# Adaptive layer norm, attention head and quantised product: the head's biases and matrices prepared elsewhere, the bias product moved, modulation rows spread from a copy

## Chip, cores and metric
One core of one Trainium2 chip. The metric is the device time of one execution in microseconds. Before the change: median 370.23 us over 3 runs (369.77 to 370.35).

## What is computed
The input x is (8, 1024, 512) in float32, eight samples of 1024 rows. The reference, cut to what matters:

```
mod = (silu(c) @ wmod).reshape(8, 6, 1, 512)
sa, ca, ga, sb, cb, gb = mod[:, 0..5]
ga, gb = sign(g) * max(|g|, 0.25) for each
h = layernorm(x) * (1 + ca) + sa
x = x + ga * attention(h)              # q, k, v, three passes, out @ Wo.T + bo
h = layernorm(x) * (1 + cb) + sb
x = x + gb * (mx_quantize(h) @ mx_quantize(weight).T + bias)
```

The attention writes only the first 16 of each sample's 1024 rows with something other than zero (before its output projection). So for all other rows the first step adds `ga * bo`, called v. The 128 first rows (16 of each of 8 samples) are "the head", and are worked apart. The quantiser divides blocks of 32 numbers by a scale and rounds each to a small grid.

## The kernel before
**Tiling.** x is handled in 16 groups of 4 tiles of 128 rows (`GROUPS`, `TILES`), two groups a sample. Tile q runs from 0 to 63. For each group: v is added (groups 0 and 1 on VectorE and GpSimd, from group 2 on by an accumulating DMA from GpSimd's queue, `sum_by_dma`, line 346); ScalarE makes sums, deviations and the normalised U (`sums`, `deviations`, `normalise`); GpSimd modulates, U * c + sb (`modulate`, lines 370 and 377, two tiles at a time); VectorE takes block maxima, quantises to Q8 and, for the early groups, multiplies back into DD (`maxima`, `block_scales`, `to_grid`, `from_grid`). TensorE turns a tile of DD (`transposes`, line 660), ScalarE copies its high part XH, VectorE subtracts the low part XL, and TensorE makes the product: the bias row first (line 675), eight matmuls with XH, four with XL. VectorE adds the result to x (`add_tile`, line 1162) and SyncE stores it. The weights are scaled by each sample's gate gb on GpSimd (`scale_weights`), turned by TensorE (`weight_turn`, line 623) at the tiles in `FOLDS` (3 to 6 for sample 1), and split into WH (ScalarE) and WL (VectorE, line 1114).

**The order.** Each engine has its queue written out by hand: the start, then `for q in range(LAST)`. At tile q TensorE does `transposes(q + 1)`, `product(q)`, `head_work(q)` and a weight turn. VectorE does `add_tile(q - 1)`, `low_part(q + 1)`, `weight_low`, the group steps that are due (`due(q, lead)`), and `head_work(q)` last. GpSimd has no tiles; it goes by group: `modulate(g)`, later `from_grid(g - 1)`, `scale_weights`, `sum_by_dma(g + 3)`.

**The start.** `silu(c)` goes to TensorE. There `spread(i, bank, signal)` multiplies a broadcast column of it with a block of wmod, so that sample 0's row of modulation stands in all 128 partitions of a PSUM bank (used for v, c and sb), and `rows_of` makes the rows of all 8 samples (8 partitions). ScalarE copies these to `msp`, and SyncE writes them to `mod_scratch` in HBM, from where later samples' rows are broadcast. c and sb of sample 0 are read by VectorE from PSUM (`first_modulate`, tiles 0 and 1) and by GpSimd from ScalarE's copies c_bc and sb_bc (tiles 2 and 3). c's rows are made inside tile 0 (`head_work(0)`), sb's at the end of the start. `gate_bias_rows` splits the bias rows of all samples into a high and low part, G, ahead of `first_modulate`.

**The head.** `head_work(q)` interleaves the head's chain. On VectorE: tile 1 makes `bias_rows` (rows of the three small layers' biases, 4 steps on one partition), tiles 2 and 3 the head's own norm, tile 4 `centre_diagonals`, which subtracts from two block-diagonal matrices in BD their mean over columns (line 948 reduction, 949 mean, 952 four 32x32 blocks each). They are first used at tile 9. On TensorE the projections to v, q and k stand in tiles 6, 7 and 8 (line 763).

Of the kernel before, what the change touches and what calls it, by code (L numbers as in the profile page):

```python
# [15 lines left out]
P = 128  # L16
# [6 lines left out]
HALF = 2  # L23
# [15 lines left out]
def build(nc, x, xh, WqT, WkT, WvT, WoT, bo, lna, BDs, rows, columns, masks, w, cT, wmod, ident, out):  # L39
# [4 lines left out]
    with ExitStack() as ctx:  # L44
# [110 lines left out]
        V_BANK, GATE_ROWS, COLUMN_ROWS, C_BANK, S_BANK, LATE_ROWS = 0, 6, 1, 2, 3, 7  # L155
# [26 lines left out]
        bd_done, hs_sa = sem("bd_done"), sem("hs_sa")  # L182
# [50 lines left out]
        def _(sp):  # L233
# [41 lines left out]
            sp.wait_ge(rows_cp, 3)  # L275
# [3 lines left out]
            sp.wait_ge(rows_cp, 4)  # L279
# [45 lines left out]
        def _(pool):  # L325
# [65 lines left out]

            add_attn_bias(1)
# [6 lines left out]
            for g in range(1, GROUPS):  # L399
# [5 lines left out]
                if g + 3 < GROUPS:  # L405
                    sum_by_dma(g + 3)
            from_grid(GROUPS - 1)

        @block.scalar
        def _(act):  # L410
# [146 lines left out]
            copy_rows(sb_rows, LATE_ROWS, 3)  # L557
# [4 lines left out]
            for q in range(LAST):  # L562
# [9 lines left out]
                if q == 1:  # L572
                    copy_rows(c_rows_all, LATE_ROWS, 4, 1.0)
# [8 lines left out]
        def _(pe):  # L582
# [3 lines left out]
            def spread(i, bank, signal):  # L586
                for k in range(NC):
                    pe.wait_ge(wmod_in[6 if i == 0 and k < HALF else i], 16)
                    m = M(ps[:, bank, :], cE[:, k, 0:1].to_broadcast([P, P]), mod_w[i][:, k, :],
                          start=k == 0, stop=k == NC - 1)  # L590
                m.then_inc(signal, 1)
# [35 lines left out]
            spread(0, V_BANK, ga_mm)  # L627
# [8 lines left out]
            spread(2, C_BANK, c_mm)  # L636
            pe.wait_ge(gb_col, 1)
            for n in range(NC):
# [3 lines left out]
            spread(3, S_BANK, s_mm)  # L642
            pe.wait_ge(blq_cp, 1)
            rows_of(3, LATE_ROWS)
# [18 lines left out]
            def product(n):  # L663
# [11 lines left out]
                M(bank, pick[:, b:b + 1].to_broadcast([P, P]), G[:], start=True, stop=False)  # L675
                pe.wait_ge(xh_done, n + 1)
                for k in range(NC):
                    r = slice(k * P, (k + 1) * P)
                    M(bank, XH[:, n % 2, r], WH[:, b % 2, k, :], start=False, stop=False)  # L679
                    M(bank, XH[:, n % 2, r], WL[:, b % 2, k, :], start=False, stop=False)  # L680
                pe.wait_ge(xl_done, n + 1)
                for k in range(NC):
                    r = slice(k * P, (k + 1) * P)
                    m = M(bank, XL[:, n % 2, r], WH[:, b % 2, k, :], start=False, stop=k == NC - 1)  # L684
                m.then_inc(y_done, 1)
# [19 lines left out]
            def attend(i, o):  # L705
                if o == 0:
# [3 lines left out]
                    if i == 0:  # L710
                        pe.wait_ge(lrow_done, 4)
                        pe.wait_ge(cleared, 5)
                        pe.wait_ge(bd_done, 1)
# [555 lines left out]
```

## Time and profile before
| what | value |
|---|---|
| median of 3 runs | 370.23 us (369.77 to 370.35) |
| the profiled execution | 371.03 us, its span 369.1 us, 6369 instructions |
| TensorE (PE) busy | 330.8 us, 90% |
| VectorE (DVE) busy | 290.8 us, 79% |
| ScalarE (ACT) busy | 223.0 us, 60% |
| GpSimd (POOL) busy | 216.9 us, 59% |
| mean granted clock of TensorE | 0.976 |
| share of the chain that ended last | PE 43%, DVE 36%, ACT 10%, issue 8% |

Times in a timeline are microseconds from the span's start. A row of a timeline gives the start, the time taken, the engine, the line of the kernel, the operation, what it writes and reads, and how many such instructions it stands for; in brackets stands how long the engine was idle before it, and what ended that. A matmul of float32 is two instructions. "Issue" in the chain is time in which an engine waited for nothing that the profile shows.

### The profile page before, as it was taken

The page shows a single profiled execution, that of the slowest core. Times are in us where ns is not written, and L with a number is a line of the kernel's source. Part 1 is how long each engine was busy: PE and PEld are TensorE (multiplying, and loading weights), DVE is VectorE, ACT ScalarE, POOL GpSimd, SP SyncE. Part 2 cuts the span into 40 slices and gives each one's busy share as a digit, 9 for nine tenths or more (in the row PEclk, how much of TensorE's full clock was granted, in tenths as well). Part 3 has the DMA queues.
Part 4 walks back from the last instruction along what each step waited for, and adds up shares of the span by engine and source line. Part 5 has one row for each costly group of instructions (what it writes and reads, how often), then busy time and mean ns, then how long its engine had stood idle before and what let it go on. Part 6 is the DMA issues. An engine that isn't in the chain of part 4 may idle for free.

```text
span 369.1 us, 6369 instructions
## 1 busy us (share of the span) xinstructions
PE 330.8 (90%) x2334; PEld 251.7 (68%) x2334; DVE 290.8 (79%) x508; ACT 223.0 (60%) x505; POOL 216.9 (59%) x131
## 2 busy tenths in 40 slices
PE   3987999549999799989999999989999989995894
PEld 1232556438988686777888678768877877684783
DVE  4799949998448996879798689896976989699732
ACT  3367654765756867786778588948593875121210
POOL 2068392462886679559967796898684767402000
PEclk9999899997999999999999999999998999998999
DMA  7989999975197727965697669768681982020122
GB/s 219 404 333 360 295 231 223 322 269 100 69 201 175 186 114 134 265 101 197 150 275 194 174 135 262 179 168 170 230 198 37 222 174 115 3 99 17 67 103 85
DMA packets 22933, 66.93 MB, mean 181 GB/s; under 512 B 2371, under 2 KB 2500, under 8 KB 18934
## 3 DMA queue, kind: packets, MB, share of 16 engines
q1 hardware_dynamic: 15360, 51.83, 41.8%
q0 software_dynamic: 7392, 14.68, 24.2%
q8 instruction: 18, 0.29, 0.3%
q14 instruction: 13, 0.11, 0.1%
q10 hardware_dynamic: 150, 0.02, 0.0%
HBM read 49.39 MB, written 17.14 MB: 180 GB/s over the span
## 4 chain that ended last, share of the span: by engine, by line
PE 43%; DVE 36%; ACT 10%; issue 8%; DMA 1%; DVEq 0%; SPq 0%; ACTq 0%
PE ps L679 7%; PE ps L680 7%; PE ps L684 7%; DVE XL L1107 5%; PE ps L660 4%; DVE Q L1148 4%; DVE WL L1114 3%; DVE amax L1129 3%; ACT U L447 3%; PE ps L763 3%; DVE X L1162 3%; PE ps L623 3%; DVE DD L1155 3%; ACT XH L430 2%; ACT unused L460 2%
## 5 line engine op out<-in xcount | busy, mean ns | idle before, releaser
L370 POOL TENSOR_TENSOR U<-U,c_bc 128x1024 f32<-128x1024 f32 x31 | 75.6, 2439 | 48.3 <-ACT U L447 48.2
L679 PE MATMUL ps<-WH,XH 128*128 128x512 f32 x256 | 103.4, 404 | 0.3 <-ACT XH L430 0.3
L680 PE MATMUL ps<-WL,XH 128*128 128x512 f32 x256 | 103.0, 402 | 0.0
L430 ACT ACTIVATE XH<-ps 128x512 fp32r<-128x512 f32 x64 | 37.8, 591 | 84.8 <-PE ps L660 84.6
L1107 DVE TENSOR_TENSOR XL<-ps,XH 128x512 fp32r<-128x512 f32 x64 | 43.9, 686 | 52.8 <-ACT XH L430 52.7
L377 POOL TENSOR_TENSOR U<-U,sb_bc 128x1024 f32<-128x1024 f32 x31 | 74.1, 2389 | 4.5 <-POOL U L370 0.2
L684 PE MATMUL ps<-WH,XL 128*128 128x512 f32 x256 | 68.8, 390 | 0.0
L447 ACT ACTIVATE U<-X,nmr,rstd 128x512 f32<-128x512 f32 x64 | 48.2, 807 | 24.7 <-DVE nmr L1122 21.5
L680 PEld LDWEIGHTS ps<-WL,XH 128*128 128x128 f32 x256 | 49.9, 195 | 11.5
L679 PEld LDWEIGHTS ps<-WH,XH 128*128 128x128 f32 x256 | 50.1, 196 | 9.5 <-ACT XH L430 0.6
L684 PEld LDWEIGHTS ps<-WH,XL 128*128 128x128 f32 x256 | 48.4, 189 | 10.5
L1162 DVE TENSOR_TENSOR X<-ps,X 128x512 f32<-128x512 f32 x64 | 43.6, 681 | 8.1 <-PE ps L684 7.8
L471 ACT ACTIVATE unused<-X,negm 128x512 bf16<-128x512 f32 x64 | 45.6, 715 | 0.5
L660 PE MATMUL ps<-idf,DD 128*128 128x128 f32 x256 | 40.0, 281 | 3.6 <-DVE WL L1114 3.1
L460 ACT ACTIVATE unused<-X 128x512 bf16<-128x512 f32 x64 | 39.4, 617 | 0.1
L1148 DVE TENSOR_TENSOR Q<-U,ps 128x1024 fp8e4<-128x1024 f32 x32 | 39.0, 1217 | 0.2
L1129 DVE TENSOR_REDUCE amax<-U 128x32 f32<-128x1024 f32 x32 | 38.7, 1209 | 0.0
L660 PEld LDWEIGHTS ps<-idf,DD 128*128 128x128 f32 x256 | 31.4, 146 | 8.3 <-DVE WL L1114 3.4
L356 POOL TENSOR_TENSOR DD<-Q,s 128x1024 f32<-128x1024 fp8e4 x12 | 23.0, 1916 | 23.4 <-DVE Q L1148 21.8
L675 PE MATMUL ps<-G,pick 128*128 128x512 f32 x64 | 31.3, 490 | 0.6 <-DVE X L1162 0.6
L346 POOL DMA_DIRECT2D X<-mod_scratch x14 | 18.5, 1325 | 17.5 <-DMA X<-in_x 12.7
L389 POOL TENSOR_SCALAR Wb<-Wd,TA 128x512 f32<-128x512 f32 x28 | 18.9, 691 | 12.8 <-PE ps L623 8.3
(219 smaller groups left out, 447.9 us busy)
## 6 DMA issues: line engine op xcount, KB each, us to landing
X<-in_x SPq DMA_DIRECT2D x16, 1024.0 KB, 8.5
out<-X SPq DMA_DIRECT2D x15, 1024.0 KB, 5.7
X<-mod_scratch POOLq DMA_DIRECT2D x14, 1024.0 KB, 12.8
X<-in_wmod SPq DMA_DIRECT2D x2, 1024.0 KB, 14.1
sb_bc<-mod_scratch SPq DMA_DIRECT2D x7, 256.0 KB, 12.1
c_bc<-mod_scratch SPq DMA_DIRECT2D x7, 256.0 KB, 10.5
X<-in_wmod SPq DMA_DIRECT2D x2, 512.0 KB, 4.7
Wd<-in_w SPq DMA_DIRECT2D x1, 1024.0 KB, 10.0
```

What stands on the lines that cost most here:

```text
L370: nc.gpsimd.tensor_tensor(a, a, spread(c_bc[:, b % 2, :]), ALU.mult).then_inc(u_done, 2 if g == 0 else 1)
L377: nc.gpsimd.tensor_tensor(a, a, spread(sb_bc[:, b % 2, :]), ALU.add).then_inc(h_done, 2 if g == 0 else 1)
L447: A.activation(U[:, g % 2, j, :], X1[:, g % XSLOTS, j, :], ACT.Identity, bias=nmr[:, g % 2, j:j + 1], scale=rstd[:, g % 2, j:j + 1]).then_ ...
L460: A.activation(unused[:, j % 2, :], X1[:, g % XSLOTS, j, :], ACT.Identity, accum_out=total[:, j:j + 1]).then_inc(sum_done, 1)
L660: m = TR(ps[:, XT_BANK + n % 2, c * P:(c + 1) * P], DD[:, j, c * P:(c + 1) * P], idf[:])
L679: M(bank, XH[:, n % 2, r], WH[:, b % 2, k, :], start=False, stop=False)
L680: M(bank, XH[:, n % 2, r], WL[:, b % 2, k, :], start=False, stop=False)
L684: m = M(bank, XL[:, n % 2, r], WH[:, b % 2, k, :], start=False, stop=k == NC - 1)
L1107: TT(XL[:, n % 2, :], ps[:, XT_BANK + n % 2, :], XH[:, n % 2, :].bitcast(F32), ALU.subtract).then_inc(xl_done, 1)
L1129: RED(amax[:, h, :], blocks(U[:, g % 2, HALF * h:HALF * (h + 1), :]), AX, ALU.max, apply_absolute_value=True).then_inc(am_done, 1)
L1148: TT(blocks(Q8[:, h]), blocks(U[:, g % 2, HALF * h:HALF * (h + 1), :]), wide(inv[:, h, :]), ALU.mult, saturate=False).then_inc(q_done, 1)
L1162: TT(a, ps[:, Y_BANK + n % 2, :], a, ALU.add).then_inc(o_done, 1)
```

## The change
- `bias_rows` moves on VectorE from tile 1 to the start, behind `early_constants`.
- `centre_diagonals` is split: VectorE makes the two means at tile 4 (`diagonal_means`), and GpSimd subtracts them, in 8 steps, behind the modulation of group 1 and the DMA for group 4, ahead of the modulation of group 2.
- A tile's bias product comes last in its sum; only tile 0 waits for G there. `gate_bias_rows` moves behind `low_part(0)`.
- The rows of c are made in the start, copied with 1 added, and sb's behind them into the same bank. c and sb of sample 0 are spread from the copies, with one matmul each.
- Banks: the column rows go from bank 1 to 7, rows of c and sb from 7 to 6. SyncE's wait for the copied rows stands once, earlier.

```diff
-            sp.wait_ge(rows_cp, 3)
+            sp.wait_ge(rows_cp, 4)
             sp.dma_start(mod_dram[SB], sb_rows).then_inc(sb_out, 16)
             sp.wait_ge(wt_mm, NC)
             sp.dma_start(Wb[:], chunked(WqT)).then_inc(wq_in, 16)
-            sp.wait_ge(rows_cp, 4)
...
+            def centre_diagonals():
+                for n, i in enumerate((0, 2)):
+                    pool.wait_ge(bdm_done, n + 1)
+                    for q in range(4):
+                        r = slice(32 * q, 32 * q + 32)
+                        nc.gpsimd.tensor_scalar(BD[r, i, r], BD[r, i, r], bdm[r, n:n + 1], 1.0,
+                                                ALU.subtract, ALU.mult).then_inc(bd_done, 1)
+                        pool.wait_ge(bd_done, 4 * n + q + 1)
...
                 if g + 3 < GROUPS:
                     sum_by_dma(g + 3)
+                if g == 1:
+                    centre_diagonals()
...
             deviations(0, 1)
+            copy_rows(c_rows_all, CS_ROWS, 3, 1.0)
             act.wait_ge(rows_turned, 1)
             A.copy(column_rows, ps[0:COLUMNS * B, COLUMN_ROWS, :]).then_inc(columns_cp, 1)
             normalise(0, 0)
+            copy_rows(sb_rows, CS_ROWS, 4)
             act.wait_ge(c_mm, 1)
-            A.activation(c_bc[:, 0, :], ps[:, C_BANK, :], ACT.Identity, bias=1.0).then_inc(c_rows, 1)
+            A.copy(c_bc[:, 0, :], ps[:, C_BANK, :]).then_inc(c_rows, 1)
             normalise(0, 1)
             act.wait_ge(s_mm, 1)
             A.copy(sb_bc[:, 0, :], ps[:, S_BANK, :]).then_inc(s_rows, 1)
             sums(1, 0)
             for k in range(NC):
                 weight_high(0, k, W_FIRST_BANKS[k])
-            copy_rows(sb_rows, LATE_ROWS, 3)
...
+            def spread(rows, bank, n, signal):
+                pe.wait_ge(rows_cp, n)
+                M(ps[:, bank, :], idf[0:B, 0:1].to_broadcast([B, P]), rows, start=True, stop=True).then_inc(signal, 1)
...
-            spread(2, C_BANK, c_mm)
+            rows_of(2, CS_ROWS)
             pe.wait_ge(gb_col, 1)
+            pe.wait_ge(blq_cp, 1)
             for n in range(NC):
                 m = TR(ps[0:COLUMNS * B, COLUMN_ROWS, n * P:(n + 1) * P],
                        TA[:, n, :, :].rearrange("p w b -> p (w b)"), idf[:])
             m.then_inc(rows_turned, 1)
-            spread(3, S_BANK, s_mm)
-            pe.wait_ge(blq_cp, 1)
-            rows_of(3, LATE_ROWS)
+            pe.wait_ge(rows_cp, 3)
+            rows_of(3, CS_ROWS)
+            spread(c_rows_all, C_BANK, 3, c_mm)
+            spread(sb_rows, S_BANK, 4, s_mm)
...
-                M(bank, pick[:, b:b + 1].to_broadcast([P, P]), G[:], start=True, stop=False)
                 pe.wait_ge(xh_done, n + 1)
...
+                if n == 0:
+                    pe.wait_ge(g_rows, 3)
+                M(bank, pick[:, b:b + 1].to_broadcast([P, P]), G[:], start=False, stop=True).then_inc(y_done, 1)
...
                 if q == 0:
                     pe.wait_ge(c_heads, 1)
                     pe.wait_ge(wt_low, NC)
-                    pe.wait_ge(rows_cp, 3)
-                    rows_of(2, LATE_ROWS)
                     head_rows(4, CA_BANK)
...
             pe.wait_ge(v_row, 1)
-            pe.wait_ge(columns_cp, 1)
-            pe.wait_ge(g_rows, 3)
+            pe.wait_ge(rows_cp, 4)
             for k in range(NC):
                 weight_turn(0, k, W_FIRST_BANKS[k])
...
-            def centre_diagonals():
+            def diagonal_means():
                 dve.wait_ge(bd_in, 16)
                 for n, i in enumerate((0, 2)):
                     link(RED(bdm[:, n:n + 1], BD[:, i, :], AX, ALU.add))
-                    link(TS(bdm[:, n:n + 1], bdm[:, n:n + 1], 1.0 / HD, None, ALU.mult))
-                    for q in range(4):
-                        r = slice(32 * q, 32 * q + 32)
-                        link(TS(BD[r, i, r], BD[r, i, r], bdm[r, n:n + 1], None, ALU.subtract))
-                W_.memset(dn[:, 4:5], 0.0).then_inc(bd_done, 1)
+                    TS(bdm[:, n:n + 1], bdm[:, n:n + 1], 1.0 / HD, None, ALU.mult).then_inc(bdm_done, 1)
...
-                STT(a, spread(C_BANK), 1.0, a, ALU.add, ALU.mult).then_inc(u_first, 1)
+                TT(a, spread(C_BANK), a, ALU.mult).then_inc(u_first, 1)
...
             early_constants()
+            bias_rows()
             first_v()
...
             quantise(Wd[:, HALF:NC, :], Q8[:, 1], HALF * NB).then_inc(wd_done, 1)
-            gate_bias_rows()
             first_modulate()
...
             low_part(0)
+            gate_bias_rows()
             maxima(0, 1)
```

## Rows read from the trace of the kernel before

**Rows 1.** The page's groups of instructions; after the bar busy us, mean ns, idle us before.
```profile
L679 PE MATMUL ps<-WH,XH 128*128 128x512 f32 x256 | 103.4, 404 | 0.3 <-ACT XH L430 0.3
...
L389 POOL TENSOR_SCALAR Wb<-Wd,TA 128x512 f32<-128x512 f32 x28 | 18.9, 691 | 12.8 <-PE ps L623 8.3
```

**Rows 2.** Chain of waits, 24 to 124 us, in order of time: start us, us, what.
```profile
28.21 0.68 DVE G L917
...
52.29 1.14 DVE amax L1129
...
55.21 1.42 DVE LR L941
...
57.37 0.46 DVE LR L941
...
58.57 0.69 DVE X L1162
```

**Rows 3.** The centring's line on VectorE: ns min/median/max, first and last start us.
```profile
L952 DVE TENSOR_SCALAR BD<-BD,bdm x8: 229/270/2320, 73.8 to 80.5; 32x32 f32<-32x32 f32 x8
```

**Rows 4.** VectorE's timeline, 73 to 89 us: start us, us, engine, line, operation.
```profile
73.34 0.27 DVE L948 TENSOR_REDUCE bdm<-BD 128x1 f32<-128x128 f32 x1
...
80.93 0.69 DVE L1162 TENSOR_TENSOR X<-ps,X 128x512 f32<-128x512 f32 x1
...
82.73 1.21 DVE L1129 TENSOR_REDUCE amax<-U 128x32 f32<-128x1024 f32 x1
...
87.89 1.22 DVE L1155 TENSOR_TENSOR DD<-Q,ps 128x1024 f32<-128x1024 fp8e4 x1
```

**Rows 5.** TensorE's timeline, 82 to 111 us, same columns.
```profile
82.96 0.45 PE L623 MATMUL ps<-idf,odd 128*128 128x128 f32 x1 [5.33 <-DVE WL L1114]
...
89.40 3.74 PE L763 MATMUL ps<-msp,early 128*128 128x128 f32 x32
...
93.41 0.60 PE L660 MATMUL ps<-idf,DD 128*128 128x128 f32 x4
...
109.91 1.08 PE L684 MATMUL ps<-WH,XL 128*128 128x512 f32 x4
```

**Rows 6.** Busy us by stretch; TensorE's granted clock stands after the POOL column.
```profile
83.00:88.00 5.00, 5.00 (x16) 4.32 (x17) 4.86 (x11) 1.09 (x2) 0.00 (x0) 0.50 0.97 178
```

**Rows 7.** TensorE's timeline, 21 to 38 us.
```profile
21.67 3.70 PE L589 MATMUL ps<-X,cE 128*128 128x512 f32 x8 [0.41 <-DMA X<-in_wmod]
...
29.18 3.60 PE L596 MATMUL ps<-U,cE 128*8 128x512 f32 x8
...
37.82 1.97 PE L660 MATMUL ps<-idf,DD 128*128 128x128 f32 x8 [3.15 <-DVE WL L1114]
```

**Rows 8.** ScalarE's timeline, a pair of normalisations and a pass of one tile.
```profile
28.23 1.50 ACT L447 ACTIVATE U<-X,nmr,rstd 128x512 f32<-128x512 f32 x2
...
99.52 0.61 ACT L460 ACTIVATE unused<-X 128x512 bf16<-128x512 f32 x1
```

**Rows 9.** VectorE's timeline, 11 to 32 us.
```profile
11.81 0.69 DVE L902 TENSOR_SCALAR odd<-ps 128x512 f32<-128x512 f32 x1 [2.88 <-PE ps L589]
...
29.63 1.22 DVE L959 SCALAR_TENSOR_TENSOR U<-ps,U 128x1024 f32<-128x1024 f32 x1
30.88 1.22 DVE L962 TENSOR_TENSOR U<-U,ps 128x1024 f32<-128x1024 f32 x1
```

**Rows 10.** GpSimd's timeline, 49 to 74 us.
```profile
49.12 2.37 POOL L377 TENSOR_TENSOR U<-U,sb_bc 128x1024 f32<-128x1024 f32 x1
...
69.24 2.35 POOL L370 TENSOR_TENSOR U<-U,c_bc 128x1024 f32<-128x1024 f32 x1 [11.66 <-ACT U L447]
71.73 2.37 POOL L377 TENSOR_TENSOR U<-U,sb_bc 128x1024 f32<-128x1024 f32 x1
```

**Rows 11.** GpSimd's timeline, its memset of one column.
```profile
1.20 0.10 POOL L327 MEMSET eps<- 128x1 f32 x1
```

**Rows 12.** The accumulating DMAs of line 346, from issue to landing.
```profile
DMA to landing us min/median/max: 9.7/12.8/19.6
```

More of the change, by code:

```diff
@@ L154, in build @@
         blq_out = bb[:, 200:201]
-        V_BANK, GATE_ROWS, COLUMN_ROWS, C_BANK, S_BANK, LATE_ROWS = 0, 6, 1, 2, 3, 7
+        V_BANK, GATE_ROWS, COLUMN_ROWS, C_BANK, S_BANK, CS_ROWS = 0, 6, 7, 2, 3, 6
         CA_BANK, SA_BANK = 6, 4
@@ L583, in _, with spread_v @@
             M, TR = nc.tensor.matmul, nc.tensor.transpose
-            def spread(i, bank, signal):
+            def spread_v():
                 for k in range(NC):
-                    pe.wait_ge(wmod_in[6 if i == 0 and k < HALF else i], 16)
-                    m = M(ps[:, bank, :], cE[:, k, 0:1].to_broadcast([P, P]), mod_w[i][:, k, :],
+                    pe.wait_ge(wmod_in[6 if k < HALF else 0], 16)
+                    m = M(ps[:, V_BANK, :], cE[:, k, 0:1].to_broadcast([P, P]), mod_w[0][:, k, :],
                           start=k == 0, stop=k == NC - 1)
-                m.then_inc(signal, 1)
+                m.then_inc(ga_mm, 1)
+            def spread(rows, bank, n, signal):
+                pe.wait_ge(rows_cp, n)
+                M(ps[:, bank, :], idf[0:B, 0:1].to_broadcast([B, P]), rows, start=True, stop=True).then_inc(signal, 1)
             def rows_of(i, bank):
@@ L626, in _ @@
             pe.wait_ge(silu_done, 1)
-            spread(0, V_BANK, ga_mm)
+            spread_v()
             rows_of(0, GATE_ROWS)
@@ L678, in product @@
                     r = slice(k * P, (k + 1) * P)
-                    M(bank, XH[:, n % 2, r], WH[:, b % 2, k, :], start=False, stop=False)
+                    M(bank, XH[:, n % 2, r], WH[:, b % 2, k, :], start=k == 0, stop=False)
                     M(bank, XH[:, n % 2, r], WL[:, b % 2, k, :], start=False, stop=False)
@@ L683, in product @@
                     r = slice(k * P, (k + 1) * P)
-                    m = M(bank, XL[:, n % 2, r], WH[:, b % 2, k, :], start=False, stop=k == NC - 1)
-                m.then_inc(y_done, 1)
+                    M(bank, XL[:, n % 2, r], WH[:, b % 2, k, :], start=False, stop=False)
+                if n == 0:
+                    pe.wait_ge(g_rows, 3)
+                M(bank, pick[:, b:b + 1].to_broadcast([P, P]), G[:], start=False, stop=True).then_inc(y_done, 1)
             def project(bank, state, dg, row, signal):
@@ L712, in attend @@
                         pe.wait_ge(cleared, 5)
-                        pe.wait_ge(bd_done, 1)
+                        pe.wait_ge(bd_done, 8)
                         pe.wait_ge(mk_in, 16)
@@ L919, in gate_bias_rows, with bias_rows @@
                 TT(G[32:32 + B, :], row, G[0:B, :].bitcast(F32), ALU.subtract).then_inc(g_rows, 1)
+            def bias_rows():
+                dve.wait_ge(cleared, 5)
+                dve.wait_ge(rows_ok, 2)
+                for r in range(2):
+                    row = lrow[0:1, r + 1, :].unsqueeze(1).to_broadcast([1, NC, P])
+                    hi, lo = (LR[n:n + 1, r, :].rearrange("p (c f) -> p c f", c=NC) for n in (0, 32))
+                    W_.tensor_copy(hi, row).then_inc(lrow_done, 1)
+                    dve.wait_ge(lrow_done, 2 * r + 1)
+                    TT(lo, row, hi.bitcast(F32), ALU.subtract).then_inc(lrow_done, 1)
             def early_constants():
@@ L933, in early_constants @@
                 link(TS(col[:, BQ:BQ + 4], col[:, BQ:BQ + 4], float(HD) ** -0.25, None, ALU.mult))
-            def bias_rows():
-                dve.wait_ge(cleared, 5)
-                dve.wait_ge(rows_ok, 2)
-                for r in range(2):
-                    row = lrow[0:1, r + 1, :].unsqueeze(1).to_broadcast([1, NC, P])
-                    hi, lo = (LR[n:n + 1, r, :].rearrange("p (c f) -> p c f", c=NC) for n in (0, 32))
-                    W_.tensor_copy(hi, row).then_inc(lrow_done, 1)
-                    dve.wait_ge(lrow_done, 2 * r + 1)
-                    TT(lo, row, hi.bitcast(F32), ALU.subtract).then_inc(lrow_done, 1)
-            def centre_diagonals():
+            def diagonal_means():
                 dve.wait_ge(bd_in, 16)
@@ L1069, in head_work @@
                 elif q == 4:
-                    centre_diagonals()
+                    diagonal_means()
                 elif q == 3:
```

7 lines of the change are left out of this document (1 added, 6 removed).

## Prediction

> **What bounds the kernel now.** I read the page first. TensorE is the busiest engine, and its first product of a tile (line 679) waited 0.3 us in 64 tiles [rows 1], so over most of the span TensorE paces the rest. Next the chain of waits, cut at 24 to 124 us, to see where it does not. From 24 us until 83 us the chain runs mainly on VectorE, with the rows of G at 28.21, the maxima of group 1 at 52.2, the head's bias rows (lines 941 and 943) from 55.21 to 58.57, and then on into the centring [rows 2]. Then the timelines. The eight centring steps of line 952 take 0.27 us in the median but 2.32 us at worst [rows 3]; with their two means they hold VectorE from 73.34 to 80.93 [rows 4]. TensorE pays: it stands idle for 5.33 us before the weight turn at 82.96 [rows 5], which waits for a subtraction queued behind the centring, and it then runs at clock 0.50, the lower level (1.2 GHz), though busy without a gap [rows 6]. From 89.40, with the value projection, it hardly pauses for several tiles. So what counts is how much sooner TensorE gets to the transposes of tile 8 (now at 93.41 [rows 5]), after which it sets the pace; the same shift then carries to the end.
>
> **The start: rows of c and sb by way of a copy.** Removed are two spreads of four matmuls (3.7 us each by the row at 21.67 [rows 7]) while c's rows, four more, move out of tile 0 to here; added are two spreads of one matmul, 0.9 us each: a matmul over 8 partitions only stands in no row, but the rows at 21.67 and 29.18 show that partitions at the output do not matter. Bounds 0.45 (were fewer rows in cheaper) and 1.8 (at clock 0.50). But the order becomes serial. In the place of the spread at 21.67 now stand c's rows, done at 25.3; ScalarE copies them out of the bank that sb's rows share, 0.6 us (a pass of 512 columns [rows 8]), beside the turning of the column rows; sb's rows then take 3.6 us [rows 7], from 25.95 to 29.55. Only behind them come the spread of c, to 30.45, and ScalarE's copy, 0.6 us, so the signal that VectorE waits for comes at 31.1. VectorE, freed at 28.2 by the rows of G moving away, starts its first modulation at 31.15 instead of 29.63 [rows 9]. ScalarE, queued behind its wait for sb's rows, next normalises two tiles (1.5 us [rows 8]) and only then copies the spread of sb: ready at 33.1. The second modulation starts at 33.1 instead of 30.88 [rows 9]: **2.2 us later**.
>
> The rows of G (28.21 to 29.63, 1.42 us [rows 2, 9]) are only moved, to behind the first low part. Ahead of that point they are paid back into the wait above; behind it they push the maxima of tile pair 2 of group 0 and the scales of group 1, which are thus **3.6 us later**. Queued on those scales are ScalarE's normalisation of group 1 and GpSimd's modulation of it, whose first half ends at 49.12 + 2.37 = 51.5 now [rows 10] and at 55.1 then. VectorE's maxima of group 1, now at 52.2, move to 55.15, **2.9 us later**. TensorE has cover in this stretch: it loses the 3.6 us of c's rows in tile 0, so its own delay is gone by tile 1. Its idle of 3.15 us before 37.82 [rows 7] becomes 3.15 + 2.2 + 1.4 = 6.7 (its weight turn starts at 31.3, 1.4 us sooner), and a slow stretch such as that of rows 6, 5 us long, may follow; the 2.5 us that it costs are covered by the missing 3.6.
>
> **The bias rows made early.** They leave 55.21 to 58.57, **3.36 us saved** [rows 2]. At their new place VectorE idles 2.88 us before 11.81 [rows 9]. The second pair of steps takes 1.2 us (57.37 to 58.57 [rows 2]); two such pairs, 2.4, fit. If the first pair's 2.16 us (a cast of 1.42) is what a first pair costs, they overrun by 0.5 us, which ends in VectorE's wait at 28 us. I take nothing, bounds 0 and 0.5. Sum so far at the maxima-to-58 us point: 2.9 - 3.36 = **0.4 us ahead**. From there the chain is VectorE's, unchanged, up to 73.34, now 72.95.
>
> **The centring on GpSimd.** VectorE keeps two reductions and two products: 2 x (0.27 + 0.04 + 0.15 + 0.04) = 1.0 us, the first from rows 4, the rest small like them. It is free at 73.95 instead of 80.93 [rows 4]. The added wait stands in GpSimd's queue **ahead of the modulation of group 2**, which today starts at 69.24 [rows 10]. It now waits for the second mean at 73.9 and for eight steps. The trace has no such step on GpSimd. From below: a memset of one column, 0.10 us [rows 11]; from above a tensor_scalar on 512 columns, 0.69 us [rows 1]; the pause between two dependent operations is 0.15 (69.24 + 2.35 to 71.73 [rows 10]). By columns 32 lie close to the small end: I take 0.14 + 0.15 = 0.29 us a step, bounds 0.25 and 0.84. The steps start at 73.45 and end at 75.8. The first half of group 2 is modulated at 75.8 + 2.35 + 0.15 + 2.37 = 80.7 [rows 10], so VectorE's maxima come at 80.75 instead of 82.73 [rows 4], **2.0 us sooner**: the centring's 7 us are mostly turned into a new wait on GpSimd.
>
> TensorE gets more. It is free at 82.96 - 5.33 - 0.4 = 77.2 [rows 5], its weight turn no longer waits and its clock stays up: turn, tile 6 and the value projection (0.4 + 3.5 + 3.7 [rows 5]) are done at 84.8. The next weight turn waits until 85.65 for VectorE; then the transposes of tile 8 need from_grid of group 2, today 87.89 + 1.22 = 89.1 [rows 4], then 87.1. They start at 87.15 instead of 93.41 [rows 5]: **6.2 us sooner**. Had TensorE alone set this, the turn behind the projection would end at 85.3: 8.1 sooner. Behind that the 6.2 us stay: GpSimd is fewer us ahead than TensorE, but VectorE asks for its group 3 only tiles after it is done.
>
> A page of the Trainium skill speaks against this move. GPSIMD Engine Reference, "Performance versus the Vector engine", has GpSimd about twice as slow as VectorE on an elementwise operation. By it a step would be 2 x 0.27 + 0.15 = 0.69 us, an estimate, and the sum 3.0 instead of 6.2. The rows have the same ratio for large operations, 2.37 us [rows 10] against 1.22 [rows 9] over 1024 columns; none has a small one on both engines, and at 32 columns I expect what an instruction costs in itself to decide.
>
> **The bias product last.** 64 instructions keep their number. In front it could have covered the wait for the high part, but that wait is 0.3 us in all [rows 1]: nothing, bound +0.3. For tile 0 it lets the product start before G is ready; G is ready 1.4 us after the first low part, which is before the product's eight high matmuls and four low ones are through. **SyncE's queue**: one wait moved forward; the rows of c and sb and the query weights leave earlier. Nobody waits for them. They compete with the addition of group 2, whose DMA itself leaves 2.6 us later from GpSimd's queue; ScalarE asks for it in tile 1, where it next waits for TensorE in any case. I take nothing, bound 2 us.
>
> **Sum**: -6.2 us. The profiled execution took 371.03 us (span 369.1), so 364.8 by its own time; it stands 0.8 above the median, so 370.23 - 6.2 = **364.0**.
>
> **Rivals.** (A) The forecast, 364.0, own range 362.5 to 365.5: **0.55**. (B) GpSimd's steps cost 0.69 us: eight of them 3.2 us more, 364.0 + 3.2 = 367.2. The step is twice VectorE's 0.27 [rows 3] and a pause of 0.15. For it: the ratio of the large operations [rows 9, 10]; against: a memset of one column takes 0.10 [rows 11], and 32 columns are few. **0.13**. (C) **Slower**: each step costs what 512 columns cost, 0.84 us. The steps end 4.4 us later, TensorE idles over 5 us before tile 8 as it does now before 82.96, and again runs 5 us or more at 0.50 [rows 6], 2.6 us lost: 364.0 + 4.4 + 2.6 = 371.0. It decides from about 0.75 us a step, where the gain is 6.2 - 3.7 - 2.6 = 0. **0.09**. (D) The start costs less and GpSimd's steps overlap more than I have it, so TensorE alone decides: 370.23 - 8.1 = 362.1. **0.13**. (E) The delay passes on through GpSimd's queue: the DMA that adds v to group 5 is issued behind group 2's second half, at 85.6 instead of 78.94. Landing takes 9.7 to 19.6 us [rows 12]. ScalarE needs it at 93.3 (today's sums at 99.52 [rows 8] less 6.2), with tile 9's high part queued behind. At 19.6 it lands at 105.2; two sums, the copy and the subtraction (1.3 + 0.6 + 0.7) make 107.8, where tile 9's last products are due at 109.91 - 6.2 = 103.7 [rows 5]: 4.1 lost, 368.1. At the median of 12.8 nothing is lost. **0.10**.
>
> **The numbers.** 364.0 is A's. The range of 361.8 to 368.0 takes in A, D and B, leaves out C and E's end. A measurement here can tell about 0.2% (0.7 us) from no change. Faster by more: A, B, D and nearly all of E, 0.84; slower: C's upper half and mishaps, 0.08; between: 0.08.
>
> **What would show it.** VectorE's first modulation starts near 31.2 after a wait on ScalarE's c_bc, the second near 33.1; group 1's maxima near 55. No LR lines at 55. GpSimd has eight small steps of about 0.14 us from 73.4 on and its group 2 at about 75.8; VectorE waits some 4 us for it before the maxima near 80.8. No idle of TensorE over 4 us from 60 to 100 us, clock 1.00 there, tile 8's transposes near 87. Wrong is the forecast if a step takes over 0.5 us, if tile 8 starts later than 89, or if the shift at 87 us is not found again at the end.

## The result, and the profile after

The changed kernel took 369.27 us in the median of 20 runs beside 371.24 for the kernel before: ratio 0.9929 (95% interval 0.9902 to 0.9956), so some 2.6 us faster. Forecast were 364.0, 6.2 us faster, range 361.8 to 368.0. The profiled execution took 368.72 us, span 366.9. The medians are over all runs; the ratio, here and below, leaves out the few slow ones (5 of the 20 of the changed kernel), so the gain is read from the ratio. Two later comparisons of the same kernel gave 0.9987 and 0.9895, so from one to the next the gain lies between 0.5 and 4 us; nowhere was it 6.

The page of the changed kernel: its busy shares, and two groups (after the bar busy us, mean ns, idle us before them):

```profile
PE 324.2 (88%) x2322; PEld 247.8 (68%) x2322; DVE 285.1 (78%) x499; ACT 223.2 (61%) x505; POOL 219.7 (60%) x139
...
L694 PE MATMUL ps<-WH,XH 128*128 128x512 f32 x256 | 108.4, 423 | 1.3 <-DVE X L1170 0.6
...
L1137 DVE TENSOR_REDUCE amax<-U 128x32 f32<-128x1024 f32 x32 | 38.7, 1210 | 8.4 <-POOL U L376 8.4
```

TensorE has 6.6 us less to do and VectorE 5.7. New is the last row: VectorE waited 8.4 us for GpSimd (line 376, the addition of sb) before its maxima. In the page of before that group had no wait. The first product of a tile waits 1.3 us in 64 tiles (0.3 before [rows 1]): the wait for VectorE's addition, which stood before the bias product, now stands before it.

VectorE's timeline, the steps that answer to [rows 4, 9] and to the chain [rows 2]:

```profile
8.96 0.42 DVE L941 CAST LR<-lrow 1x512 fp32r<-1x512 f32 x1
...
10.57 0.68 DVE L943 TENSOR_TENSOR LR<-lrow,LR 1x512 fp32r<-1x512 f32 x1
...
32.71 1.22 DVE L969 TENSOR_TENSOR U<-ps,U 128x1024 f32<-128x1024 f32 x1 [4.04 <-ACT c_bc L563]
34.60 1.22 DVE L972 TENSOR_TENSOR U<-U,ps 128x1024 f32<-128x1024 f32 x1 [0.67 <-ACT sb_bc L566]
...
56.70 1.22 DVE L1137 TENSOR_REDUCE amax<-U 128x32 f32<-128x1024 f32 x1 [2.40 <-POOL U L376]
...
74.48 0.28 DVE L962 TENSOR_REDUCE bdm<-BD 128x1 f32<-128x128 f32 x1
...
83.91 1.22 DVE L1137 TENSOR_REDUCE amax<-U 128x32 f32<-128x1024 f32 x1 [5.95 <-POOL U L376]
```

The bias rows end at 11.25, inside the old idle time. The first modulation waits 4.04 us for ScalarE's copy of c and starts at 32.71 (now against 29.63 before), the second at 34.60 (30.88). Group 1's maxima stand at 56.70 (52.2), behind 2.40 us of waiting for GpSimd. The means are made at 74.5, and then the maxima of group 2 wait 5.95 us for GpSimd: they come at 83.91, **later** than before the change (82.73).

GpSimd's timeline, for [rows 10], and TensorE's, for [rows 5, 7]:

```profile
75.06 3.80 POOL L397 TENSOR_SCALAR BD<-BD,bdm 32x32 f32<-32x32 f32 x8 [12.28 <-DVE bdm L963]
78.94 2.39 POOL L369 TENSOR_TENSOR U<-U,c_bc 128x1024 f32<-128x1024 f32 x1
81.47 2.40 POOL L376 TENSOR_TENSOR U<-U,sb_bc 128x1024 f32<-128x1024 f32 x1
```

```profile
23.05 3.60 PE L611 MATMUL ps<-X,cE 128*8 128x512 f32 x8 [0.55 <-DMA X<-in_wmod]
...
27.33 3.60 PE L611 MATMUL ps<-U,cE 128*8 128x512 f32 x8
30.86 1.98 PE L606 MATMUL ps<-msp,idf 8*128 8x512 f32 x4
...
41.54 1.97 PE L677 MATMUL ps<-idf,DD 128*128 128x128 f32 x8 [6.80 <-DVE WL L1122]
...
84.03 3.73 PE L780 MATMUL ps<-msp,early 128*128 128x128 f32 x32
...
90.44 0.63 PE L677 MATMUL ps<-idf,DD 128*128 128x128 f32 x4 [0.86 <-DVE DD L1163]
```

The eight centring steps take 3.80 us, and group 2's modulation starts behind them, at 78.94 instead of 69.24. TensorE begins the value projection at 84.03 instead of 89.40 and the transposes of tile 8 at 90.44 instead of 93.41, 3.0 us sooner. At the end 2.2 us are left of that (spans of 366.9 and 369.1).

### The profile page after: what moved, and what is told of

It is laid out like the page before. It is cut to its first block, busy times and chain, and to the rows that moved or that the text cites. A ratio compares the mean times of both kernels' runs of the same rounds, so it can differ in the third digit from the quotient of the medians.

```text
span 366.9 us, 6399 instructions
## 1 busy us (share of the span) xinstructions
PE 324.2 (88%) x2322; PEld 247.8 (68%) x2322; DVE 285.1 (78%) x499; ACT 223.2 (61%) x505; POOL 219.7 (60%) x139
## 4 chain that ended last, share of the span: by engine, by line
PE 43%; DVE 28%; ACT 10%; issue 8%; DMA 4%; POOL 3%; SPq 2%; DVEq 0%; ACTq 0%; POOLq 0%
PE ps L694 8%; PE ps L695 8%; PE ps L699 7%; PE ps L677 5%; DMA X<-in_wmod 4%; DVE XL L1115 4%; DVE amax L1137 4%; DVE Q L1156 3%; ACT U L458 3%; DVE WL L1122 3%; DVE DD L1163 3%; PE ps L638 2%; DVE X L1170 2%; ACT XH L441 2%; PE ps L611 2%
## 5 line engine op out<-in xcount | busy, mean ns | idle before, releaser
L694 PE MATMUL ps<-WH,XH 128*128 128x512 f32 x256 | 108.4, 423 | 1.3 <-DVE X L1170 0.6
L702 PE MATMUL ps<-G,pick 128*128 128x512 f32 x64 | 25.2, 393 | 0.0
```

The lines of the kernel that those rows point to most:

```text
L694: M(bank, XH[:, n % 2, r], WH[:, b % 2, k, :], start=k == 0, stop=False)
```

## Experiments

A kernel that is said to run "beside" another ran on the same chip; all others are compared by their ratios to the kernel before, each on its own chip. "c's rows" are the four matmuls (eight instructions) that stand at 23.05 above; their start says how late the start of the kernel ran.

### What differs from run to run

The kernel before, profiled once more:

> The kernel before, once more, for a second profile. It is there to tell how much of the shift of the start is the change and how much differs from run to run: in the changed kernel's profile the DMA of the third block of wmod, which releases TensorE at 23.05 us, came 1.4 us later than in the profile of before (21.67), although nothing in the change comes ahead of it. If this is run-to-run, this profile and the next one of the changed kernel both show values between 21.5 and 23.5 with no order. If the change caused it (bias rows on VectorE or another order of loads), this one is near 21.7 and the changed kernel near 23.0. Tile 8's transposes at 93 to 95 us, 5.3 us of TensorE idle before 83.

Its span was 366.8 us, 2.3 less than in the profile that the forecast worked from. TensorE's timeline of this second profile of before, and the stretches 70 to 80 and 80 to 90 us of it and then of the first profile (granted clock behind the POOL column):

```profile
22.98 3.70 PE L589 MATMUL ps<-X,cE 128*128 128x512 f32 x8 [0.52 <-DMA X<-in_wmod]
...
83.25 0.30 PE L623 MATMUL ps<-idf,odd 128*128 128x128 f32 x1 [3.75 <-DVE WL L1114]
...
87.14 3.74 PE L763 MATMUL ps<-msp,early 128*128 128x128 f32 x32
...
91.15 0.60 PE L660 MATMUL ps<-idf,DD 128*128 128x128 f32 x4
```

```profile
70.00:80.00 10.00, 6.44 (x26) 4.82 (x25) 9.65 (x16) 8.86 (x25) 9.71 (x5) 0.83 0.84 312
80.00:90.00 10.00, 6.75 (x47) 6.24 (x48) 9.66 (x20) 4.24 (x10) 0.55 (x2) 1.00 0.90 203
```

```profile
70.00:80.00 10.00, 4.72 (x25) 3.61 (x25) 9.61 (x16) 9.11 (x25) 9.71 (x5) 1.00 0.80 302
80.00:90.00 10.00, 7.04 (x27) 6.08 (x28) 9.69 (x19) 4.00 (x9) 0.55 (x2) 0.66 0.81 192
```

Two things are no property of the kernel. The third block of wmod released TensorE at 22.98, not at 21.67; VectorE's first modulation nevertheless stood at 29.83 (29.63), and group 1's maxima, though the second modulation came 0.7 us later (31.61), at 52.0 (52.2). And the slow stretch of the clock lay at 70 to 80, where TensorE waits anyway, instead of 80 to 90: VectorE's maxima of group 2 stood where they were (83.02 against 82.73), but tile 8's transposes came at 91.15 instead of 93.41. The forecast had counted its 6.2 us from 93.41, so it had booked that slow stretch (2.6 us by its own figure, 2.3 by the two profiles) as a gain of the change. Against this profile the changed kernel gained 0.7 us at tile 8.

The changed kernel, on two more chips:

> The changed kernel, once more, on the chip of the next runs. Expected ratio 0.993 to before. Theory A (the centring steps on GpSimd, 0.475 us each, stand ahead of the modulation of group 2 and VectorE's maxima wait for it): VectorE again waits near 6 us for GpSimd before the maxima of group 2, tile 8's transposes start at 90 to 90.5 when the start is late (23.05) and near 89 when it is early. Theory B (the gain was lost at the start, in the DMA or the serial rows): the wait for GpSimd varies with the start and the ratio with it.

> The changed kernel a third time, beside e12 on the same chip. Two comparisons so far gave 0.9929 and 0.9987; expected 0.993 to 0.999, and the start of c's rows on TensorE between 22.9 and 24.6 us, with VectorE's first modulation 9.65 us behind it, as in the seven profiles of this start.

Medians 370.87 and 368.92, ratios 0.9987 (0.9955 to 1.0020) and 0.9895 (0.9854 to 0.9935). Expected were 0.993 and 0.993 to 0.999, so both ratios miss, one to each side. c's rows began at 24.12 and 24.77, the first modulation at 33.77 and 34.42, each 9.65 us behind. VectorE waited 5.24 and 5.29 us for GpSimd, and tile 8 came at 91.57 and 92.17.

### The place of the centring

Behind group 2's modulation instead of ahead of it:

```diff
-                if g == 1:
+                if g == 2:
                     centre_diagonals()
...
                     pe.wait_ge(kT_ready, i + 1)
+                    if i == 0:
+                        pe.wait_ge(bd_done, 8)
                     M(ba, BD[:, 0, :], qT, start=True, stop=True).then_inc(qc_mm, 1)
```

> The centring on GpSimd moved behind the modulation of group 2, and TensorE's wait for it ahead of its first use. Theory A: GpSimd starts group 2 at about 70 us instead of 79, VectorE's wait of 6 us before the maxima goes, and TensorE alone sets tile 8: with the start as late as in the changed kernel's profile its transposes begin at 88.0 instead of 90.4, so 2.4 us faster than the changed kernel, ratio to before near 0.987. Theory B: under 0.5 us, since the loss lies ahead of 60 us. Theory C (GpSimd's work collides with VectorE's on the shared memory port, wherever it stands): VectorE's steps of groups 1 and 2 grow by over 1 us and the gain is under 1 us.

Median 367.06, 3.8 us below the changed kernel beside it; ratio 0.9880 (0.9841 to 0.9919). GpSimd's, VectorE's and TensorE's timelines of this kernel:

```profile
70.79 2.35 POOL L369 TENSOR_TENSOR U<-U,c_bc 128x1024 f32<-128x1024 f32 x1 [7.60 <-ACT U L458]
```

```profile
79.07 1.21 DVE L1138 TENSOR_REDUCE amax<-U 128x32 f32<-128x1024 f32 x1
```

```profile
88.52 0.60 PE L677 MATMUL ps<-idf,DD 128*128 128x128 f32 x4
```

Group 2's modulation started at 70.79, the maxima at 79.07 without a wait, tile 8 at 88.52, with c's rows at 23.44. So GpSimd's wait was what held tile 8, as theory A has it. The port theory falls for these steps: between 64 and 90 us VectorE's subtractions of the low part took 684 and 686 ns in the mean in the changed kernel and in this one, its quantising steps 1218 in both and its maxima 1216 and 1212.

In the kernel before, the centring alone, ahead of group 2 as in the change (the GpSimd function and its wait as in the change's diff, all else as before):

> The kernel before with the centring alone moved to GpSimd, ahead of group 2's modulation as in the change. Theory A: VectorE makes its means near 73.6 us, GpSimd's eight steps of 0.475 us end near 78, group 2's first half is modulated near 83 and the maxima of group 2 come at 83.0, exactly where the two profiles of before have them (82.7 and 83.0): VectorE's saving of 7 us is fully turned into a wait of some 6 us. TensorE still gains, tile 8's transposes near 89.5 against 91 to 93.4 before, so 1.5 us faster without a slow stretch of the clock and up to 3.9 with one: ratio 0.990 to 0.996. Rival (what the deleted steps cost is simply gained): 6 us, ratio 0.984.

Median 368.23, ratio 0.9931 (0.9897 to 0.9966). VectorE's, GpSimd's and TensorE's timelines of this kernel:

```profile
72.78 0.28 DVE L960 TENSOR_REDUCE bdm<-BD 128x1 f32<-128x128 f32 x1
...
82.18 1.22 DVE L1137 TENSOR_REDUCE amax<-U 128x32 f32<-128x1024 f32 x1 [6.02 <-POOL U L377]
```

```profile
73.36 3.80 POOL L398 TENSOR_SCALAR BD<-BD,bdm 32x32 f32<-32x32 f32 x8 [16.34 <-DVE bdm L961]
77.24 2.39 POOL L370 TENSOR_TENSOR U<-U,c_bc 128x1024 f32<-128x1024 f32 x1
```

```profile
80.75 3.74 PE L775 MATMUL ps<-msp,early 128*128 128x128 f32 x32
87.23 0.30 PE L635 MATMUL ps<-idf,odd 128*128 128x128 f32 x1 [2.74 <-DVE WL L1122]
...
88.72 1.09 PE L672 MATMUL ps<-idf,DD 128*128 128x128 f32 x4 [0.86 <-DVE DD L1163]
```

7 us of centring are off VectorE, and it waits 6.02 us: maxima at 82.18 against 82.73 and 83.02. The gain is all of TensorE's, which no longer idles before the turn that stood at 83 and has the value projection done by 84.5; 3.6 us of that lead are then spent in waiting, 2.74 and 0.86, ahead of tile 8.

The same kernel with the centring behind group 2 (the diff of the first run of this section):

> The kernel before with the centring on GpSimd behind group 2's modulation and nothing else. It stands beside e8 to tell what the early bias rows are worth once the centring is out of the way. Theory A: 0.8 us, since VectorE's next low part waits for tile 3's copy at 58.3 us in any case: ratio 0.980 to 0.985. Rival: 3.36 us, their full length: ratio 0.988.

Median 364.12, ratio 0.9815 (0.9774 to 0.9856): **this one move gives 6.9 us (1.85% of 371), more than twice the whole change.** GpSimd and TensorE in it:

```profile
69.88 2.36 POOL L370 TENSOR_TENSOR U<-U,c_bc 128x1024 f32<-128x1024 f32 x1 [11.83 <-ACT U L459]
...
80.37 4.32 POOL L398 TENSOR_SCALAR BD<-BD,bdm 32x32 f32<-32x32 f32 x8
```

```profile
84.81 3.74 PE L776 MATMUL ps<-msp,early 128*128 128x128 f32 x32
...
88.82 0.60 PE L672 MATMUL ps<-idf,DD 128*128 128x128 f32 x4
```

No single profile shows all 6.9 us. Tile 8 came at 88.82, level with the 88.72 of the kernel with the centring ahead of group 2, though that one's VectorE had begun its first modulation 1.1 us sooner (29.46 against 30.56). The difference shows one tile on: tile 9's transposes came at 97.09 with the centring ahead and at 95.80 with it behind; in the former the waits of 2.74 and 0.86 us were followed by a granted clock of 0.57 from 88 to 92, in the latter it was 1.00 there. That is 1.3 us, 2.4 counted from the first modulation; the spans of the two profiles differ by 1.9, the ratios by 1.2% (4.3 us). Where the rest comes in was not found.

### What a step on GpSimd costs

```diff
-                    for q in range(4):
-                        r = slice(32 * q, 32 * q + 32)
+                    for q in range(8):
+                        r = slice(32 * (q // 2), 32 * (q // 2) + 32)
+                        c = slice(16 * q, 16 * q + 16)
-                        nc.gpsimd.tensor_scalar(BD[r, i, r], BD[r, i, r], bdm[r, n:n + 1], 1.0,
+                        nc.gpsimd.tensor_scalar(BD[r, i, c], BD[r, i, c], bdm[r, n:n + 1], 1.0,
```

> The changed kernel with each of GpSimd's eight steps of 32 columns cut into two of 16, so the same elements in sixteen steps. If the 0.475 us of a step (0.39 and the pause) belong to the instruction, the steps take 7.5 us instead of 3.8, VectorE's maxima of group 2 come 3.7 us later (near 88) and the kernel is slower than the changed one by 3 to 4 us: ratio to before 1.003 to 1.008. If they belong to the columns (the page's and rivals' way: GpSimd twice as slow as VectorE), 16 half steps take what 8 do and the ratio stays 0.993 to 0.999.

The tile BD on GpSimd, in the changed kernel and then in this one (ns min/median/max, first and last start):

```profile
L397 POOL TENSOR_SCALAR BD<-BD,bdm x8: 387/389/402, 75.1 to 78.5; 32x32 f32<-32x32 f32 x8
```

```profile
L398 POOL TENSOR_SCALAR BD<-BD,bdm x16: 341/345/355, 76.8 to 83.4; 32x16 f32<-32x16 f32 x16
```

Half the columns save some 45 ns of 389. So, as an estimate from these two sizes, 0.30 us belong to the instruction and 0.09 to the 32 columns; with the pause before the next, a step is 0.475 us. Median 373.65, ratio 1.0085 (1.0052 to 1.0118). Against the changed kernel's 0.9929 (0.9932 for the one that ran beside it with the bias product first, told of below) that is 1.5%, more than the 3.1 us by which group 2's maxima moved (88.72 less 24.76 for c's rows, against 83.91 less 23.05): TensorE then idled 4.25 us before a turn near 94 and had the clock at 0.83 from 90 to 100.

### The early bias rows

```diff
             early_constants()
+            bias_rows()
             first_v()
...
-                elif q == 1:
-                    bias_rows()
```

> The kernel before with the bias rows alone made early. Theory A: they leave 3.36 us of VectorE at 55 us, but its next low part waits for tile 3's transposes and copy (58.3 us), so only 0.8 us arrive at 59 us and at the end: ratio 0.998. Rival (my forecast's arithmetic, 3.36 us saved in full): ratio 0.991.

Median 370.42, ratio 0.9998 (0.9969 to 1.0027). VectorE's timeline of it:

```profile
55.52 0.68 DVE L1160 TENSOR_TENSOR X<-ps,X 128x512 f32<-128x512 f32 x1
58.73 0.69 DVE L1105 TENSOR_TENSOR XL<-ps,XH 128x512 fp32r<-128x512 f32 x1 [2.54 <-ACT XH L430]
59.34 1.21 DVE L1153 TENSOR_TENSOR DD<-Q,ps 128x1024 f32<-128x1024 fp8e4 x1
```

The 3.4 us freed at 55 us turn into 2.54 us of waiting for the high part of tile 3, which TensorE and ScalarE make no sooner. What arrives is 0.4 us at 59.34 (59.77 before). In the full change they do shorten the chain, since there everything ahead of 57 us is late: with the steps put back (the next run) this low part came 41.3 us behind c's rows, against 37.3 in the changed kernel. The four steps are also cheaper at their new place: 2.3 us (8.96 to 11.25) instead of 3.36, since the first cast took 0.42 us there and 1.42 beside GpSimd's modulation [rows 2].

### The start

The changed kernel with bias rows and centring as before:

> The changed kernel with bias rows and centring put back as before: what is left is the serial start by copies, the rows of G behind the first low part, the bias product last and the banks. Theory A: group 1's maxima come 3.5 to 4.7 us later than in the kernel before (55.5 to 57.5 against 52.1), and so does VectorE's chain through the bias rows and the centring: slower by 3 to 4.5 us, ratio 1.008 to 1.012. Rival: TensorE's saving of 3.6 us in tile 0 makes up for it, ratio 1.000.

Median 376.40, ratio 1.0161 (1.0121 to 1.0201): **the new start, with the rows of G behind it, loses 6 us**, more than the 3 to 4.5 expected. (The bias product last is in it too, and is worth nothing, as told below.) c's rows began at 24.28 here. The maxima of group 1 came at 57.92 and those of group 2 at 89.17, 6.4 later than in the kernel before.

Only the rows of G, put back to their place ahead of the first modulation in the changed kernel:

```diff
             quantise(Wd[:, HALF:NC, :], Q8[:, 1], HALF * NB).then_inc(wd_done, 1)
+            gate_bias_rows()
             first_modulate()
...
             low_part(0)
-            gate_bias_rows()
             maxima(0, 1)
```

> The rows of G back ahead of VectorE's first modulation, where in the changed kernel it waits 4.0 us for ScalarE's copy of c, so that they cost nothing there. Theory A (all delays in front of GpSimd's modulation of group 1 are passed on, through the maxima of group 1, to tile 8): group 1's maxima 1.4 us earlier, and tile 8 too: 1.4 us faster than the changed kernel, ratio to before near 0.989. Rival: the delay is swallowed between 57 and 84 us by the waits for GpSimd; then under 0.3 us.

Median 368.45 against 370.87 beside it, ratio 0.9915 (0.9881 to 0.9950). Counted from c's rows, group 1's maxima came 1.4 us sooner and tile 8's transposes 0.7 (66.8 against 67.5 us behind them), half of what was expected; the medians differ by 2.4, more than this move explains. With both repairs, centring later and G early:

> The changed kernel with both repairs: centring behind group 2's modulation, rows of G ahead of VectorE's first modulation. Theory A: the two add up, 2.4 to 3.6 and 1.4 us: group 1's maxima near 55.6, no wait for GpSimd before group 2's, the value projection near 83.1 against 84.5 with the first repair alone; ratio to before 0.983 to 0.985. Rival: once GpSimd's wait is gone TensorE sets tile 8 from further back and the second repair gives nothing: ratio 0.988 as with the first alone.

Median 366.49, ratio 0.9890 (0.9839 to 0.9940). Counted from c's rows, group 1's maxima again 1.4 us sooner than with the first repair alone, tile 8 only 0.2 (64.9 against 65.1). Here the rival holds: once GpSimd is out of the way, the place of G gives nothing that can be measured.

Late data, by loading two blocks of wmod earlier in the changed kernel:

```diff
+            load_mod(1)
             sp.dma_start(Wd[:], w.rearrange("(c p) k -> p c k", p=P)).then_inc(w_in, 16)
-            load_mod(1)
+            load_mod(2)
             load_x(1)
-            load_mod(2)
             load_mod(3)
```

> The changed kernel with two blocks of wmod loaded earlier: block 1 ahead of the weights, block 2 ahead of group 1 of x. Theory A (the serial start passes every microsecond of late data on to VectorE): TensorE starts c's rows at 21.2 to 22.0 instead of 22.9 to 24.6, VectorE's first modulation 9.65 us behind it, at 30.9 to 31.6, group 1's maxima near 55 and tile 8's transposes near 88.7: 1.5 to 2 us faster than the changed kernel beside it, ratio of the two 0.995. Rival (loads are not what the start waits for, or the weights come too late then): no gain or a loss.

It ran beside the changed kernel's third comparison. Median 367.92 against 368.92; ratios to before 0.9856 (0.9811 to 0.9901) and 0.9895. TensorE's and VectorE's timelines of it:

```profile
21.94 3.60 PE L611 MATMUL ps<-X,cE 128*8 128x512 f32 x8
```

```profile
31.59 1.23 DVE L969 TENSOR_TENSOR U<-ps,U 128x1024 f32<-128x1024 f32 x1 [2.50 <-ACT c_bc L563]
```

c's rows 2.8 us sooner than in the run beside it (24.77), the first modulation again 9.65 behind them, tile 8 at 89.35 instead of 92.17. Not all of the 2.8 is the loads': in the run beside it the matmuls ahead of c's rows ran at a granted clock of 0.50, which made 1.1 us of it (see **Open** in the section after next), so the loads gave 1.7. The 2.8 us arrive whole at tile 8, but by tile 9 they are 1.2 (97.96 against 99.17), as this kernel had a slow stretch there and the other had none. The time shows 1.0, with intervals too wide to tell the two apart. The same loads in the kernel with the old start:

> The same earlier loads in the kernel with the start of before (that of e8, ratio 0.983). Theory A: there VectorE starts its first modulation at 29.5 to 29.9 whether the data come at 21.7 or at 23.0, so the earlier loads give nothing: 0.979 to 0.986 as e8. Rival: they help here as much as in the changed kernel, ratio 0.978.

Median 365.74, ratio 0.9817 (0.9773 to 0.9860), as without them (next section). TensorE had its data by 22.02, and the first modulation came at 30.45, later than the 29.5 to 29.9 expected: VectorE was busy without a gap from its first step for v at 12.63 (11.81 before) on. So in the old start VectorE's own queue sets that moment, not the loads.

### The order of the bias product, and the best version

The bias product first again, but for tile 0, in the changed kernel:

```diff
+                if n:
+                    M(bank, pick[:, b:b + 1].to_broadcast([P, P]), G[:], start=True, stop=False)
                 pe.wait_ge(xh_done, n + 1)
```

> The changed kernel with the bias product first again in every tile but tile 0. Theory A: TensorE's first product of a tile does not wait, so the order is worth nothing: the same as the changed kernel within the interval, 0.993 to 0.999 to before. Rival: in front, the product covered the turn from transposes to products and let VectorE's addition start 0.2 us sooner; then faster than the changed kernel by up to 1 us.

Median 368.79, ratio 0.9932 (0.9897 to 0.9966), the same as the changed kernel's 0.9929: worth nothing either way.

The old start, order of G and bias product, with the bias rows early and the centring behind group 2, built from the diffs above:

> The kernel before with the bias rows early and the centring on GpSimd behind group 2's modulation, but with its own start, rows of G and bias product. Theory A (the start is what the change loses, the place of the centring the rest): group 1's maxima near 51.5 us, GpSimd starts group 2 near 69, no wait for it, the value projection near 80.8 and the query projection near 88 (93.5 with the centring ahead of group 2's modulation, 94.6 to 96.8 in the kernel before): ratio 0.978 to 0.983, the best of all. Rival (what is gained by 90 us is given back later, as TensorE runs ahead of GpSimd and the DMAs of the next groups): ratio 0.987 to 0.990, with new idle time of TensorE between 90 and 125 us.

Median 364.39, ratio 0.9829 (0.9790 to 0.9868). With the centring later alone it was 364.12 beside it. These two beat both kernels. The rival, that the lead is lost after 90 us, does not hold: no wait of TensorE stands between 83 and 120 us in either. The value projection of the first was at 83.16, later than the 80.8 expected. The waits ahead of it are gone; what is late is the clock: it was 0.50 from 74 to 78 us, and from tile 6's transposes (73.47) to the value projection TensorE took 9.7 us, where the kernel with the centring ahead of group 2, at full clock, took 7.3.

## Why the prediction was wrong

**The bound and the mechanism of the centring: right.** The 7 us off VectorE came back as a wait for GpSimd, in the change (5.95 us) and with the centring alone (6.02). The forecast had seen it, at some 4 us. Of its three signs of being wrong one struck: tile 8 at 90.44, later than 89. A step stayed just under 0.5 us, and most of the shift at tile 8 was found again at the end.

**The step that failed first: the price of a step on GpSimd.** I took 0.14 + 0.15 = 0.29 us, from a memset of one column. It measured 0.39 + 0.09, so 3.80 us for eight where 2.35 were booked: 1.5 us. The half steps show that at this size neither the ratio of the engines nor the columns decide, but a cost of the instruction itself of some 0.30 us. The page of the Trainium skill named in the forecast (GPSIMD Engine Reference, "Performance versus the Vector engine") has its factor of about two from an addition of two tensors over 2048 columns; the forecast's estimate of 0.69, drawn from it, was too much beside the measured 0.475. The rows had a closer pair: a tensor_scalar on 512 columns took 0.69 us on both engines [rows 1, 9], VectorE's reading from PSUM, so for this kind of step the factor of two did not hold even there. Rival B had named the right place with too dear a price; no rival named the start.

**The second: the start.** "31.15 instead of 29.63" was 32.71. The length of the serial chain was right: from c's rows to the first modulation 9.48 us by the forecast, 9.65 or 9.66 in nine of the ten profiles of the new start, and 10.08 in the one with the bias rows put back. Its beginning was not: I set it at 21.67, as in the profile of before, where nothing hung on that moment. The old start has slack behind it (21.67 and 22.98 give 29.63 and 29.83, and group 1's maxima at 52.2 and 52.0); in the new one it is the head of the chain, and in the profiles it lay between 22.95 and 24.77. At group 1's maxima this made 4.5 us of delay instead of 2.9, at the point where the bias rows give back 3.4: behind by 1.1 us, not ahead by 0.4.

**The two together** are 3.0 of the 3.3 us that are missing at tile 8 (90.44 against 87.15).

**The third: the clock.** Some 2.3 us of the gain were the slow stretch before 89 us, which the profile of before happened to have and its second profile had elsewhere. Nor did the change end such stretches: where the forecast had the clock at 1.00 from 60 to 100 us, the changed kernel's own profile has 0.83 from 70 to 80. This does not show as an error between the two profiles, but it does between the medians: what one execution shows of the clock was taken as a property of the kernel.

**What else was right, and what was not said.** TensorE's idle time before the first transposes was 6.80 us, by the forecast 6.7, and it was covered as foreseen: tile 1's transposes came at 50.55 against 50.20 before. The 3.36 us of the bias rows were real only because the start was late; alone they are worth nothing (ratio 0.9998), which the forecast did not say. The bias product at zero was right (0.9932 against 0.9929), as was that nobody waits for SyncE's queue. The lead of 3.0 us at tile 8 was 2.2 at the end. From the key projection to the last low products TensorE took 259.3 us in the profile of before and 259.9 in the one after, but 259.0 and 262.1 in two more profiles of the changed kernel, so the 0.8 us lie within what its executions differ by.

**Open.** c's rows began on average later in profiles of the new start (22.95 to 24.77, nine of them without the changed loads) than the matmuls at their place did with the old one (21.67 to 23.17, six). Part of it is the clock. In five of the nine the matmuls ahead of them, the product with the second block, took 5.30 us instead of 3.60, at a granted clock of 0.50, and in none of the six. Where they took 3.60, c's rows began 5.20 to 5.25 us behind the start of these matmuls, in old and new start alike; where they took 5.30, 6.31 or 6.32 us behind it. So the slow clock made 1.1 us in those five, and without it the nine would lie between 22.95 and 23.7, against 21.67 to 23.17. The rest is the arrival of the second block. Nothing ahead of either is changed that I can see, and the ranges overlap; whether the change causes them was not settled.

## What to carry to other kernels

Work taken off a busy engine is worth what the next wait on that engine leaves of it: place it on the other engine behind what the first will ask for next. The same eight steps, in the kernel before, gave 2.6 us (0.9931) ahead of group 2's modulation and 6.9 us (0.9815) behind it. When a step becomes the head of a serial chain, take the latest start that it can have, not the one that a profile shows while nothing hung on it. And profile the kernel before twice before booking a slow stretch of the clock.

## What was not expected of the hardware

- A tensor_scalar of GpSimd on a 32x32 block took 389 ns and on 32x16 345 ns, where VectorE's median for 32x32 was 270 [rows 3]: by an estimate from the two sizes, 0.30 us are fixed.
- TensorE's granted clock was 0.50 from 83 to 88 us in one profile of the kernel before, and in the other the slow stretch lay between 74 and 78 us, though the two waits of TensorE ahead of 74 us were alike (1.82 and 1.23 us, 1.83 and 1.23). Tile 8 came 2.3 us later in the one.
- The same loads, issued in the same order, released TensorE at times 1.5 us apart (21.67 to 23.17) in six profiles of kernels whose start on TensorE is the same.
- What VectorE and GpSimd cost each other shows in the kernel before: a centring step on VectorE took up to 2.32 us beside GpSimd's operations of 2.37, and 0.27 in the median [rows 3, 10]. With the centring back on VectorE and the new start, four steps took 5.22 us beside GpSimd's modulation and four 1.19 beside nothing but its issue of a DMA. The first cast of the bias rows took 0.42 us at the start, and 1.42 and 2.08 in the two kernels where GpSimd was modulating. The additions, subtractions and maxima of VectorE did not grow (above). The Trainium skill (SBUF — State Buffer, "Who interferes with whom") has the two engines share a pair of ports, which one holds for a whole instruction while the other is blocked, where VectorE's step is of a kind that uses both of its pairs, as a tensor_scalar or a cast can; by that rule a short step waits out a long one, and these rows agree.
- GpSimd's steps were not always alike: with the centring behind group 2, in the kernel before, one of GpSimd's eight steps took 0.92 us and the median step 0.39, so the eight took 4.32 us instead of 3.80. What held that one was not looked into.
